# First feed-forward of a four-layer gated block: steps in another order, and w1 applied to inputs split into three bf16 planes

## The chip, the cores and the metric

The kernel runs on one core of one Trainium2 chip. The metric is the device time of one execution of the whole program, in microseconds. The core's engines work from queues of their own and meet at semaphores: TensorE (PE; its weight loads are listed as PEld), VectorE (DVE), ScalarE (ACT), GpSimd (POOL) and SyncE (SP).

## The reference, cut to what matters

The program is four layers, each a cross-attention and a feed-forward, on `x` of 4 x 1024 x 256 in f32. The change lies in the feed-forward of layer 0, which quantises its inputs to 8 bits, its weights to -1, 0 and 1, and has a convolution over three neighbouring positions between its two products:

```python
def act_quant(x):
    scale = 127.0 / jnp.clip(jnp.max(jnp.abs(x), axis=-1, keepdims=True), 1e-05)
    return jnp.clip(jnp.round(x * scale), -128, 127) / scale

def weight_quant(w):
    scale = 1.0 / jnp.clip(jnp.mean(jnp.abs(w)), 1e-05)
    return jnp.clip(jnp.round(w * scale), -1, 1) / scale

def bit_linear(x, w):
    xq = x + jax.lax.stop_gradient(act_quant(x) - x)
    wq = w + jax.lax.stop_gradient(weight_quant(w) - w)
    return jnp.einsum('bsd,hd->bsh', xq, wq)
...
h = bit_linear(x, w1)                                   # 256 -> 1024
h = depthwise_conv1d(h.transpose(0, 2, 1), conv_w, conv_b)   # over positions
...                                                     # silu
return bit_linear(h, w2)                                # 1024 -> 256
...
x = x + jnp.tanh(g_ffn[0]) * _L0_ffn_ref(_layernorm(x, axis=-1), L0_ffn_w1, L0_ffn_conv_w, L0_ffn_conv_b, L0_ffn_w2)
```

## The kernel before, in words

The program runs stage after stage. The one changed is `stage_l0_ffn` (from L213), which runs from about 184 to 453 us. It works through B = 4 batches of 1024 positions (S), each of TB = 8 row tiles of 128 positions, T = 32 tiles in all. The hidden size of 1024 is cut into M = 8 slices of 128. A slot g (0 to 31) is one slice of one batch: b = g // 8, m = g % 8.

What is done to a slot, with hidden channels on the partitions and positions along the row:
- `up(g, half)` (L372, PE): the slice of w1 (128x128, f32, kept as f32 though its values are -1, 0, 1) against the turned inputs `xt` (f32), 512 positions a half, into the PSUM bank `hb[g % 2]`.
- `centre(g)` (L471, ACT): the middle tap of the convolution and its bias, 1024 columns. `conv(g, tap)` (L304 and L306, DVE): the two outer taps, 1023 columns each. `silu(g)` (L477, ACT): into ring buffer `z` of 16 slots.

What is done to a tile t, one tile per step and LAG = 9 steps behind the slots, so that all eight slices of its batch are there:
- `turn_z(t)` (L388, PE): eight 128x128 transposes into PSUM. `largest_hidden(t)` (L311 to L316, DVE): the largest absolute value of each row, and two scales from it. `quantise(t, half)` (L483, ACT): four slices each into `zq`, rounded by adding a large constant.
- `turn_back(t, half)` (L402, PE): four transposes. `copy_q(t, half)` (L490, ACT): to bf16 in `q2`. `down(t)` (L414, PE): eight bf16 matmuls of 256 columns with w2. `update(t)` (L321, DVE): onto the residual. `stats(t)` (L209, DVE): sums for the next layer norm.

What prepares the inputs of the next batch, beside the slots of this one: in slots m < 4 `norm` (L449, ACT) and `largest_input` (L278, DVE), two tiles a step; in slots m >= 4 `quantise_x` (L456, ACT), `dequantise` (L291, DVE), `turn_x` (L362, PE), `copy_x` (L463, ACT), two tiles a step. For batch 0 these run ahead of the first slot, followed on DVE by `norm_range` (L146 to L153), the mean and the reciprocal deviation of the other 24 tiles. `turn_x`, `turn_back` for half 0 and for half 1 share one PSUM bank, `back`.

Each engine runs its list of calls step by step, written out by hand in the loops at the end of its block; an engine never runs anything ahead of its list. In a step of index g the slot g is put through `up`, slot g - 1 through `centre`, `conv` and `silu`; tile t = g - 9 is turned, and tile t - 1 turned back and multiplied by w2. From tile TAIL = 24 on no slots are left (the drained tail, steps 33 to 42); there tiles alternate between two sets of PSUM banks, and PE does `turn_z(t)` ahead of `turn_back(t-1)`:

```python
if 0 <= t - 1 < T:
    copy_q(t - 1, 0)
    copy_q(t - 1, 1)
...
if 0 <= t < T:
    quantise(t, 0)
    quantise(t, 1)
```

This is ScalarE's order around the change. GpSimd has nothing to do in this stage. `round_weights` (L799), in the program's first stage, rounds w1 to -1, 0, 1.

## Time and profile before

| | |
|---|---|
| median of 3 runs | 1910.52 us (1905.21, 1910.52, 1912.49) |
| profiled execution | 1910.83 us, span in the profile 1909.0 us |
| granted TensorE clock, mean | 0.942 |
| busy over the span | PE 1644.5 us (86%), DVE 1159.0 (61%), ACT 882.7 (46%), POOL 321.8 (17%) |
| the changed stage | about 184 to 453 us |

A time is in microseconds from the start of the span. A row of a list names the engine, the line of the code, the operation, the tile written, the tiles read and their shapes; "x8" is eight instructions listed as one. In square brackets stands how long the engine had been idle and what released it. f32 matmuls of 512 columns stand with two records each. The clock that the chip grants TensorE is given as a share of its full 2.4 GHz; 0.50 is the lower level of 1.2 GHz.

### The profile page before, as it was taken

What the parts mean: (1) busy time and instruction counts of PE and PEld (TensorE: products, weight loads), DVE (VectorE), ACT (ScalarE), POOL (GpSimd) and SP (SyncE); (2) the same over time, 40 slices, a digit from 0 to 9 for tenths busy, and PEclk for the clock granted to TensorE, in tenths of its full rate; (3) what the DMA queues carried; (4) which work ended last, traced back from release to release, by engine and by line L of the source; (5) the groups of instructions that cost most, each with busy time, mean ns of one, the idle gap of its engine ahead of it and who ended that gap; (6) DMA issues with size and microseconds to landing.
All of it is one profiled execution on the core that took longest, in us unless ns stands there. A gap on an engine that the chain in (4) does not pass through costs nothing. (4 is left out here: it accounts for less than half of the span.)

```text
span 1909.0 us, 29587 instructions
## 1 busy us (share of the span) xinstructions
PE 1644.5 (86%) x10149; PEld 1246.8 (65%) x10149; DVE 1159.0 (61%) x2579; ACT 882.7 (46%) x1795; POOL 321.8 (17%) x359
## 2 busy tenths in 40 slices
PE   7797788887899898799997399999936999979998
...
GB/s 200 1 1 1 1 1 1 1 1 127 1 1 1 1 1 1 31 1 1 2 1 195 291 65 73 73 70 73 70 196 28 1 2 1 2 47 1 0 1 89
DMA packets 62849, 78.83 MB, mean 41 GB/s; under 512 B 13179, under 2 KB 52655, under 8 KB 62319
## 3 DMA queue, kind: packets, MB, share of 16 engines
...
## 5 line engine op out<-in xcount | busy, mean ns | idle before, releaser
L3002 PEld LDWEIGHTS moe_bank<-moe_xt,moe_w1e 128*128 128x128 f32 x1264 | 155.0, 194 | 5.7 <-DVE moe_xt L2850 1.8
L3002 PE MATMUL moe_bank<-moe_xt,moe_w1e 128*128 128x128 f32 x1264 | 155.8, 277 | 1.1 <-DVE moe_xt L2850 1.1
L3012 PE MATMUL moe_bank<-moe_w,moe_xin 128*128 x632 | 149.3, 379 | 0.0
L3076 ACT ACTIVATE moe_xin<-moe_bank,moe_b 128x128 f32<-128x128 f32 x316 | 90.3, 368 | 124.9 <-PE moe_bank L3002 124.9
L372 PE MATMUL l0f_hb<-l0f_xt,f_w 128*128 128x512 f32 x256 | 125.7, 623 | 5.3 <-DVE l0f_a L306 3.8
L1471 POOL TENSOR_TENSOR all_x<-all_x,l1x_fbias 128x256 f32<-128x256 f32 x32 | 23.3, 732 | 589.9 <-DVE l1x_fxn L204 589.9
L3012 PEld LDWEIGHTS moe_bank<-moe_w,moe_xin 128*128 128x128 f32 x632 | 114.0, 190 | 12.3
L209 DVE BATCH_NORM_STATS2 all_stats<-all_x 128x6 f32<-128x256 f32 x256 | 104.0, 421 | 5.2
L2859 DVE TENSOR_TENSOR moe_y<-moe_bank,moe_b2r 128x256 f32<-128x256 f32 x79 | 33.5, 424 | 118.8 <-PE moe_bank L3012 118.8
L2919 POOL DMA_INDIRECT moe_results<-moe_y,moe_row x79 | 78.0, 988 | 125.1 <-DVE moe_y L2859 121.8
L2850 DVE COPY moe_xt<-moe_bank 128x256 f32<-128x256 f32 x79 | 33.5, 424 | 106.6 <-PE moe_bank L2990 106.6
L2086 PE MATMUL l3f_bank<-l3f_xt,l3f_wx 128*128 128x512 f32 x192 | 87.8, 608 | 0.0
L3067 ACT ACTIVATE moe_w1e<-moe_w 128x1024 f32 x79 | 83.4, 1057 | 3.2 <-issue 2.0
L2914 POOL DMA_INDIRECT moe_xin<-moe_inputs,moe_token x79 | 76.8, 972 | 26.3 <-PE moe_bank L2990 21.6
L2526 PE MATMUL l3x_o_bank<-l3x_vrow,l3x_pt 128*128 128x136 f32 (+1 forms) x640 | 81.2, 282 | 0.0
L2526 PE MATMUL l2x_o_bank<-l2x_vrow,l2x_pt 128*128 128x136 f32 (+1 forms) x640 | 80.6, 281 | 0.0
L372 PEld LDWEIGHTS l0f_hb<-l0f_xt,f_w 128*128 128x128 f32 x256 | 46.9, 200 | 48.4 <-issue 46.3
L2526 PEld LDWEIGHTS l3x_o_bank<-l3x_vrow,l3x_pt 128*128 128x128 f32 (+1 forms) x640 | 77.3, 191 | 0.4
L304 DVE SCALAR_TENSOR_TENSOR l0f_a<-l0f_hb,l0f_cw,l0f_a 128x1023 f32<-128x1023 f32 x32 | 41.0, 1282 | 59.4 <-ACT l0f_a L471 59.4
L2526 PEld LDWEIGHTS l2x_o_bank<-l2x_vrow,l2x_pt 128*128 128x128 f32 (+1 forms) x640 | 76.4, 190 | 0.5
L2164 ACT ACTIVATE l3f_gate<-l3f_bank,l3f_cols 128x512 f32<-128x512 f32 x36 | 24.7, 687 | 105.4 <-PE l3f_bank L2094 105.4
L2008 DVE TENSOR_TENSOR l3f_prod<-l3f_gate,l3f_ct 128x512 f32<-128x512 f32 x12 | 8.3, 692 | 94.4 <-ACT l3f_gate L2164 94.4
...
## 6 DMA issues: line engine op xcount, KB each, us to landing
...
```

The lines of the kernel that those rows point to most:

```text
L209: return nc.vector.bn_stats(sh.stats[:, ds(t * 6, 6)], x_tile(sh, t))
L304: k.link(nc.vector.scalar_tensor_tensor(a[:, u, 1:S], h[:, 0:S - 1], cw[:, m, 0:1], a[:, u, 1:S], ALU.mult, ALU.add))
L372: ins = nc.tensor.matmul(hb[g % 2][:, half * 512:(half + 1) * 512], w1[:, d, m * P:(m + 1) * P], xt[:, b % 2, d, half * 512:(half + 1) * 5 ...
L2086: ins = nc.tensor.matmul(bank[3 * m + k][:, :], wx[:, k, c, m * P:(m + 1) * P], xt[:, c, b * S + j * G:b * S + (j + 1) * G], start=(c == 0 ...
L2526: ins = nc.tensor.matmul(o_bank[:, m * VW:(m + 1) * VW], pt[0:rows(i), u, n, j * P:(j + 1) * P], vrow[0:rows(i), ds((t // TB) * (DC * NV * ...
L2850: nc.vector.tensor_copy(xt[:, u, :], bank[3 * u][:, 0:D]).then_inc(s.et_ready, 1)
L2914: nc.gpsimd.indirect_dma_start(out=gathered(t), out_offset=None, in_=xnd, in_offset=bass.IndirectOffsetOnAxis(ap=token[:, t:t + 1], axis=0 ...
L2919: nc.gpsimd.indirect_dma_start(out=ys, out_offset=bass.IndirectOffsetOnAxis(ap=row[:, t:t + 1], axis=0), in_=y[:, u, :], in_offset=None).t ...
L3002: ins = nc.tensor.matmul(out, w1e[:, at:at + P], xt[:, u, c * P:(c + 1) * P], start=(c == 0), stop=(c == DC - 1))
L3012: ins = nc.tensor.matmul(bank[4 + u][:, 0:D], ht[:, u, c * P:(c + 1) * P], w2[:, ds(e * (HC * D) + c * D, D)], start=(c == 0), stop=(c == ...
L3067: nc.scalar.activation(w1e[:, u * DC * HID:(u + 1) * DC * HID], w1[:, ds(e * (DC * HID), DC * HID)], ACT.Copy).then_inc(s.w1e_ready, 1)
L3076: ins = nc.scalar.activation(ht[:, u, m * P:(m + 1) * P], bank[1 + u][:, m * P:(m + 1) * P], ACT.Gelu, bias=b1[:, ds(e * HC + m, 1)])
```

## The change

- w1 is rounded into a bf16 tile `w1b` (`round_weights`).
- The turned inputs go to `xt` as f32 (now one buffer for one batch) and are split exactly into three bf16 planes `xs`: the rounded value, the rounded rest, the rest of the rest. `up` does six bf16 matmuls a half (two slices of the inputs by three planes), and waits for its own half of the planes.
- Batch 0 is split by ACT (first plane beside the copy, `middle`) and DVE (`rest`, `low`), ahead of `norm_range`; the other twelve pairs of tiles by GpSimd, four operations each, in a chain.
- A step now turns back and multiplies tile t - 2 in place of t - 1 on PE, `turn_z(t)` stands at the end of the step, and there is one step more. `zq` has two buffers. DVE begins a step with `largest_hidden(t-1)`, and `update` and `stats` work on t - 3. ACT has `centre` ahead of `quantise_x`, and `quantise(t-1)` between the two `copy_q(t-2)`.

The diff, cut to its core:

```diff
+        xt = s.sb("xt", [P, DC, S])
+        xs = s.sb("xs", [P, 2, 3, DC, S], BF16)
+        zq = s.sb("zq", [P, 2, 2, HM * P])
...
+                def rest(t):
+                    dve.wait_ge(s.xt_ready, t + 2)
+                    nc.vector.tensor_tensor(rows(t), rows(t), plane(t, 0), ALU.subtract).then_inc(s.rest_ready, 2)
+
+                def low(t):
+                    dve.wait_ge(s.mid_ready, t + 2)
+                    nc.vector.tensor_tensor(plane(t, 2), rows(t), plane(t, 1), ALU.subtract).then_inc(s.xs_ready, 2)
+
                 for t in range(TB):
                     dequantise(t)
+                for t in range(0, TB + 2, 2):
+                    if t < TB:
+                        rest(t)
+                    if t >= 2:
+                        low(t - 2)
                 norm_range(nc, c, sh, TB, T)
...
-                for g in range(END + 3):
+                for g in range(END + 4):
...
-                    if 0 <= t - 2 < T:
-                        update(t - 2)
+                    if 0 <= t - 1 < T:
+                        largest_hidden(t - 1)
+                    if 0 <= t - 3 < T:
+                        update(t - 3)
                     if 1 <= g <= SLOTS:
                         conv(g - 1, 0)
                         conv(g - 1, 1)
...
-                    if 0 <= t < T:
-                        largest_hidden(t)
...
+            @block.gpsimd
+            def _(pool):
+                k = Chain(pool, s.split_step)
+                for t in range(TB, T, 2):
+                    pool.wait_ge(s.xt_ready, t + 2)
+                    if t % TB == 0 and t >= 2 * TB:
+                        pool.wait_ge(s.h_ps, (t // TB - 1) * M)
+                    k.link(nc.gpsimd.tensor_copy(plane(t, 0), rows(t)))
+                    k.link(nc.gpsimd.tensor_tensor(rows(t), rows(t), plane(t, 0), ALU.subtract))
+                    k.link(nc.gpsimd.tensor_copy(plane(t, 1), rows(t)))
+                    nc.gpsimd.tensor_tensor(plane(t, 2), rows(t), plane(t, 1), ALU.subtract).then_inc(s.xs_ready, 2)
...
                 def up(g, half):
                     b, m = g // M, g % M
+                    pe.wait_ge(s.xs_ready, b * TB + (half + 1) * TB // 2)
                     if half == 0:
-                        pe.wait_ge(s.xt_ready, (b + 1) * TB)
                         if g >= 2:
                             pe.wait_ge(s.conv_ready, g - 1)
                     for d in range(DC):
-                        ins = nc.tensor.matmul(hb[g % 2][:, half * 512:(half + 1) * 512], w1[:, d, m * P:(m + 1) * P],
-                                               xt[:, b % 2, d, half * 512:(half + 1) * 512], start=(d == 0), stop=(d == DC - 1))
+                        for k in range(3):
+                            ins = nc.tensor.matmul(hb[g % 2][:, half * 512:(half + 1) * 512], w1[:, d, m * P:(m + 1) * P],
+                                                   xs[:, b % 2, k, d, half * 512:(half + 1) * 512],
+                                                   start=(d == 0 and k == 0), stop=(d == DC - 1 and k == 2))
...
-                    if t > TAIL and t < T:
-                        turn_z(t, 0)
-                        turn_z(t, 1)
-                    if 0 <= t - 1 < T:
-                        turn_back(t - 1, 0, fed)
+                    if 0 <= t - 2 < T:
+                        turn_back(t - 2, 0, fed)
                     if g < SLOTS:
                         up(g, 0)
-                    if 0 <= t - 1 < T:
-                        turn_back(t - 1, 1, fed)
-                    if 0 <= t <= TAIL:
-                        turn_z(t, 0)
-                        turn_z(t, 1)
+                    if 0 <= t - 2 < T:
+                        turn_back(t - 2, 1, fed)
                     if g < SLOTS:
                         up(g, 1)
                     if b < B - 1 and m >= HM:
-                        turn_x(fed, max(0, 2 * t))
+                        turn_x(fed, max(0, 2 * (t - 1)))
                         fed += 2
-                    if 0 <= t - 1 < T:
-                        down(t - 1)
+                    if 0 <= t - 2 < T:
+                        down(t - 2)
+                    if 0 <= t < T:
+                        turn_z(t, 0)
+                        turn_z(t, 1)
...
                 def copy_x(t):
                     act.wait_ge(s.xt_ps, t + 2)
+                    if t < TB:
+                        nc.scalar.activation(pair(plane(t, 0)), turned(t), ACT.Copy)
+                    else:
+                        act.wait_ge(s.xs_ready, t - TB + 2)
+                    nc.scalar.activation(pair(rows(t)), turned(t), ACT.Copy).then_inc(s.xt_ready, 2)
+
+                def middle(t):
+                    act.wait_ge(s.rest_ready, t + 2)
+                    nc.scalar.activation(plane(t, 1), rows(t), ACT.Copy).then_inc(s.mid_ready, 2)
...
+                    if 1 <= g <= SLOTS:
+                        centre(g - 1)
                     if b < B - 1 and m >= HM:
                         quantise_x((b + 1) * TB + 2 * (m - HM))
                         quantise_x((b + 1) * TB + 2 * (m - HM) + 1)
-                    if 1 <= g <= SLOTS:
-                        centre(g - 1)
+                    if 0 <= t - 2 < T:
+                        copy_q(t - 2, 0)
                     if 0 <= t - 1 < T:
-                        copy_q(t - 1, 0)
-                        copy_q(t - 1, 1)
+                        quantise(t - 1, 0)
+                        quantise(t - 1, 1)
+                    if 0 <= t - 2 < T:
+                        copy_q(t - 2, 1)
...
-                    nc.vector.tensor_scalar(f.w1[:, :, :], f.w1[:, :, :], -1.0, None, ALU.max)
+                    nc.vector.tensor_scalar(f.w1b[:, :, :], f.w1[:, :, :], -1.0, None, ALU.max)
```

How this moves instructions, at three places. Names: `l0f_zt` and `l0f_hb0` hold a turned tile, `l0f_back` and `l0f_hb1` the one turned back, `l0f_q2` is what `down` reads.

ScalarE in the drained tail, before: both `copy_q` (L490) of a tile stand ahead of the two `quantise` (L483) of the next.

```order
L490 ACTIVATE l0f_q2<-l0f_back 128x512
L490 ACTIVATE l0f_q2<-l0f_hb1 128x512
L483 ACTIVATE l0f_zq<-l0f_zt,l0f_sc2 128x512 x2
L490 ACTIVATE l0f_q2<-l0f_back 128x512
L490 ACTIVATE l0f_q2<-l0f_hb1 128x512
L483 ACTIVATE l0f_zq<-l0f_hb0,l0f_sc2 128x512 x2
```

After:

```order
L533 ACTIVATE l0f_q2<-l0f_back 128x512
L526 ACTIVATE l0f_zq<-l0f_zt,l0f_sc2 128x512 x2
L533 ACTIVATE l0f_q2<-l0f_hb1 128x512
L533 ACTIVATE l0f_q2<-l0f_back 128x512
L526 ACTIVATE l0f_zq<-l0f_hb0,l0f_sc2 128x512 x2
L533 ACTIVATE l0f_q2<-l0f_hb1 128x512
```

The second `copy_q` of a tile has moved behind the `quantise` of the next tile.

VectorE in a step with inputs (m >= 4), before: the taps (L304, L306), `dequantise` (L291), `largest_hidden` (L311 to L316), `stats` and `update`.

```order
L304 SCALAR_TENSOR_TENSOR l0f_a<-l0f_hb0,l0f_cw,l0f_a 128x1023
L306 SCALAR_TENSOR_TENSOR l0f_a<-l0f_hb0,l0f_cw,l0f_a 128x1023
L291 TENSOR_SCALAR f0_xn<-f0_xn,f0_inv1 128x256 x2
L311 TENSOR_REDUCE l0f_am2<-l0f_zt 128x1
L313 TENSOR_SCALAR l0f_am2<-l0f_am2 128x1
L315 RECIPROCAL l0f_sc2<-l0f_am2 128x1
L316 TENSOR_SCALAR l0f_inv2<-l0f_am2,f0_wmean 128x1
L209 BN_STATS all_stats<-all_x 128x6
L321 SCALAR_TENSOR_TENSOR all_x<-l0f_yb,l0f_inv2,all_x 128x256
```

After:

```order
L333 TENSOR_REDUCE l0f_am2<-l0f_zt 128x1
L335 TENSOR_SCALAR l0f_am2<-l0f_am2 128x1
L337 RECIPROCAL l0f_sc2<-l0f_am2 128x1
L338 TENSOR_SCALAR l0f_inv2<-l0f_am2,f0_wmean 128x1
L343 SCALAR_TENSOR_TENSOR all_x<-l0f_yb,l0f_inv2,all_x 128x256
L326 SCALAR_TENSOR_TENSOR l0f_a<-l0f_hb0,l0f_cw,l0f_a 128x1023
L328 SCALAR_TENSOR_TENSOR l0f_a<-l0f_hb0,l0f_cw,l0f_a 128x1023
L300 TENSOR_SCALAR f0_xn<-f0_xn,f0_inv1 128x256 x2
L209 BN_STATS all_stats<-all_x 128x6
```

`largest_hidden` (L333 to L338) has moved ahead of the taps (L326, L328) and works on the tile turned in the step before.

VectorE at the opening of the stage, before: the eight `dequantise`, then `norm_range`.

```order
L291 TENSOR_SCALAR f0_xn<-f0_xn,f0_inv1 128x256 x8
L146 TENSOR_TENSOR all_var<-all_stats 128x24
```

After:

```order
L300 TENSOR_SCALAR f0_xn<-f0_xn,f0_inv1 128x256 x8
L304 TENSOR_TENSOR l0f_xt<-l0f_xt,l0f_xs 128x2x256 x2
L308 TENSOR_TENSOR l0f_xs<-l0f_xt,l0f_xs 128x2x256
L304 TENSOR_TENSOR l0f_xt<-l0f_xt,l0f_xs 128x2x256
L308 TENSOR_TENSOR l0f_xs<-l0f_xt,l0f_xs 128x2x256
L304 TENSOR_TENSOR l0f_xt<-l0f_xt,l0f_xs 128x2x256
L308 TENSOR_TENSOR l0f_xs<-l0f_xt,l0f_xs 128x2x256 x2
L146 TENSOR_TENSOR all_var<-all_stats 128x24
```

`rest` (L304) and `low` (L308) of four pairs stand between the two.

## Rows read from the trace of the kernel before

**Rows 1.** The costly groups by form, stage alone, 184 to 452.8 us.

```profile
L372 PE MATMUL l0f_hb<-l0f_xt,f_w 128*128 128x512 f32 x256 | 125.7, 623 | 5.3 <-DVE l0f_a L306 3.8 <-ACT l0f_xt L463 1.5
```

**Rows 2.** In order of time (start, duration): `centre` of five slots, last statistics.

```profile
199.00 1.20 ACT L471 ACTIVATE l0f_a<-l0f_hb,l0f_cb,l0f_cw 128x1024 f32<-128x1024 f32 x1 [0.77 <-PE l0f_hb L372]
...
240.98 1.20 ACT L471 ACTIVATE l0f_a<-l0f_hb,l0f_cb,l0f_cw 128x1024 f32<-128x1024 f32 x1
...
300.05 1.22 ACT L471 ACTIVATE l0f_a<-l0f_hb,l0f_cb,l0f_cw 128x1024 f32<-128x1024 f32 x1
...
360.16 1.21 ACT L471 ACTIVATE l0f_a<-l0f_hb,l0f_cb,l0f_cw 128x1024 f32<-128x1024 f32 x1
...
412.74 1.20 ACT L471 ACTIVATE l0f_a<-l0f_hb,l0f_cb,l0f_cw 128x1024 f32<-128x1024 f32 x1
...
452.34 0.43 DVE L209 BATCH_NORM_STATS2 all_stats<-all_x 128x6 f32<-128x256 f32 x1
```

**Rows 3.** The same list, a step without inputs.

```profile
312.20 1.27 ACT L483 ACTIVATE l0f_zq<-l0f_zt,l0f_sc 128x512 f32<-128x512 f32 x2 [0.41 <-DVE l0f_sc L315]
...
312.94 0.65 PE L402 MATMUL l0f_back<-all_ident,l0f_zq 128*128 128x128 f32 x4 [0.25 <-ACT l0f_zq L483]
...
314.59 1.28 DVE L304 SCALAR_TENSOR_TENSOR l0f_a<-l0f_hb,l0f_cw,l0f_a 128x1023 f32<-128x1023 f32 x1 [0.88 <-ACT l0f_a L471]
...
317.11 1.22 DVE L311 TENSOR_REDUCE l0f_am<-l0f_zt 128x1 f32<-128x1024 f32 x1
...
318.74 0.68 DVE L278 TENSOR_REDUCE f_am<-f_xn 128x2 f32<-128x512 f32 x1
318.75 1.26 ACT L483 ACTIVATE l0f_zq<-l0f_zt,l0f_sc 128x512 f32<-128x512 f32 x2 [0.41 <-DVE l0f_sc L315]
```

**Rows 4.** The same list, a step with inputs.

```profile
343.46 0.91 ACT L456 ACTIVATE f_xn<-f_xn,f_sc 128x256 f32<-128x256 f32 x2
...
348.02 0.61 DVE L291 TENSOR_SCALAR f_xn<-f_xn,f_inv 128x256 f32<-128x256 f32 x2
...
350.63 0.48 DVE L321 SCALAR_TENSOR_TENSOR all_x<-l0f_yb,l0f_inv,all_x 128x256 f32<-128x256 f32 x1
```

**Rows 5.** The same list, the drained tail.

```profile
434.44 1.04 PE L388 MATMUL l0f_zt<-all_ident,l0f_z 128*128 128x128 f32 x8
...
436.45 0.59 ACT L490 ACTIVATE l0f_q<-l0f_hb 128x512 bf16<-128x512 f32 x1
...
437.16 1.26 ACT L483 ACTIVATE l0f_zq<-l0f_zt,l0f_sc 128x512 f32<-128x512 f32 x2
437.18 1.03 PE L414 MATMUL l0f_hb<-f_w2q,l0f_q 128*128 128x256 bf16 x8 [0.83 <-ACT l0f_q L490]
...
438.05 1.04 PE L388 MATMUL l0f_hb<-all_ident,l0f_z 128*128 128x128 f32 x8
```

**Rows 6.** The same list, first and last operation of `norm_range` at the opening.

```profile
187.91 0.19 DVE L146 TENSOR_TENSOR all_var<-all_stats 128x24 f32<-128x24 f32 x1
...
191.60 0.18 DVE L153 SCALAR_TENSOR_TENSOR all_shift<-all_mean,all_rstd 128x24 f32<-128x24 f32 x1
```

**Rows 7.** Lines of GpSimd in other stages: duration in ns, min/median/max.

```profile
L886 POOL COPY l0x_rhs<-l0x_crest x4: 607/608/636, 39.6 to 49.4; 128x512 f32<-128x512 f32 x4
...
L2067 POOL TENSOR_TENSOR l3f_prod<-l3f_gate x16: 1263/1768/1772, 1715.9 to 1870.4; 128x512 f32<-128x512 f32 x16
```

**Rows 8.** A pause; two stretches: PE, PEld, DVE, ACT, POOL busy, granted clock.

```profile
226.73 0.63 PE L362 MATMUL l0f_back<-all_ident,f_xn 128*128 128x128 f32 x4 [2.45 <-DVE f_xn L291]
...
226.00:232.00 6.00, 5.27 (x12) 2.42 (x12) 2.58 (x5) 3.54 (x5) 0.00 (x0) 0.72 0.00 0
...
432.00:440.00 8.00, 6.31 (x55) 5.48 (x53) 5.72 (x13) 5.14 (x9) 0.00 (x0) 1.00 0.00 1
```

**Rows 9.** In order of time, GpSimd and VectorE together, in layer 1.

```profile
752.44 0.72 POOL L1471 TENSOR_TENSOR all_x<-all_x,l1x_fbias 128x256 f32<-128x256 f32 x1 [0.44 <-DVE l1x_fxn L204]
...
752.56 0.63 DVE L148 TENSOR_TENSOR all_mean<-all_stats 128x8 f32<-128x8 f32 x1
```

More of the change, by code:

```diff
@@ L228, in stage_l0_ffn @@
         norm_sems(s)
-        w1, w2, w2q, wscale, wmean = f.w1, f.w2, f.w2q, f.wscale, f.wmean
+        w1, w2, w2q, wscale, wmean = f.w1b, f.w2, f.w2q, f.wscale, f.wmean
         xn, am, sc, inv1 = f.xn, f.am, f.sc, f.inv1
@@ L248, in stage_l0_ffn, with rows, plane @@
         tg = sh.gates[:, 4:5]
+        def rows(t):
+            j = t % TB
+            return xt[:, :, j * P:(j + 2) * P]
+        def plane(t, k):
+            b, j = t // TB, t % TB
+            return xs[:, b % 2, k, :, j * P:(j + 2) * P]
         def z_bank(t):
@@ L344, in _ @@
                             input_scales(b + 1)
-                    if 0 <= t - 2 < T:
-                        stats(t - 2)
+                    if 0 <= t - 3 < T:
+                        stats(t - 3)
                     if g == 2:
@@ L401, in turn_back @@
                     for i in range(HM):
-                        ins = nc.tensor.transpose(back_bank(t, half)[:, i * P:(i + 1) * P], zq[:, half, i * P:(i + 1) * P], sh.ident[:, :])
+                        ins = nc.tensor.transpose(back_bank(t, half)[:, i * P:(i + 1) * P], zq[:, t % 2, half, i * P:(i + 1) * P], sh.ident[:, :])
                     ins.then_inc(s.back_ps, 1)
@@ L456, in quantise_x, with turned, pair @@
                     nc.scalar.activation(xn[:, j, :], xn[:, j, :], ACT.Copy, bias=MAGIC, scale=sc[:, j:j + 1]).then_inc(s.q1_ready, 1)
+                def turned(t):
+                    return back[:, :].rearrange("p (t c n) -> p t c n", t=2, n=P)
+                def pair(ap):
+                    return ap.rearrange("p c (t n) -> p t c n", n=P)
                 def copy_x(t):
-                    b, j = t // TB, t % TB
                     act.wait_ge(s.xt_ps, t + 2)
-                    if b >= 2 and j == 0:
-                        act.wait_ge(s.h_ps, (b - 1) * M)
-                    nc.scalar.activation(xt[:, b % 2, :, j * P:(j + 2) * P].rearrange("p c (t n) -> p t c n", n=P),
-                                         back[:, :].rearrange("p (t c n) -> p t c n", t=2, n=P), ACT.Copy).then_inc(s.xt_ready, 2)
+                    if t < TB:
[6 more added lines that the diff above has]
+                    nc.scalar.activation(plane(t, 1), rows(t), ACT.Copy).then_inc(s.mid_ready, 2)
                 def centre(g):
@@ L494, in _ @@
                     quantise_x(t)
-                for t in range(0, TB, 2):
-                    copy_x(t)
+                for t in range(0, TB + 2, 2):
+                    if t < TB:
+                        copy_x(t)
+                    if t >= 2:
+                        middle(t - 2)
                 act.wait_ge(s.small_loaded, 32)
@@ L516, in _ @@
                         silu(g - 1)
-                    if 0 <= t < T:
-                        quantise(t, 0)
-                        quantise(t, 1)
                     if b < B - 1 and m >= HM:
```

15 lines of the change are left out of this document (7 added, 8 removed).

## The prediction

> **What bounds the kernel now.** I first asked the table of costly groups restricted to the stage (184.3 to 452.8 us) what the changed matmuls amount to: 256 f32 records of w1, 125.7 us [rows 1]. The change takes work from these, so the question is whether TensorE sets the time. The list in order of time says it does not. The `centre` starts [rows 2] cut the stage into batches: 199.00 (slot 0), 240.98 (slot 7), 300.05 (slot 15), 360.16 (slot 23), 412.74 (slot 31); the last statistics end at 452.34 + 0.43 = 452.77. Inside a plain step [rows 3] the loop runs through ScalarE and VectorE: `quantise` at 312.20 on ScalarE and `centre` behind it, two `conv` taps on VectorE from 314.59, `largest_hidden` at 317.11, the next `quantise` at 318.75: 6.55 us a step. TensorE waits in it: `turn_back` starts at 312.94 after 0.25 us idle for `zq`. Its own work (two `turn_back` of about 0.45, two halves of `up` of 1.71 = 4 x 0.43, `turn_z` 0.87, `down` 0.87, the last two by the starts in rows 5) is 6.0 of the 6.55. In the drained tail [rows 5] nothing of `up` is left, and a tile takes 438.05 - 434.44 = 3.61 us. I cost the change by the loops it leaves.
>
> **Part 1: bf16 planes in `up`.** Four records of 0.43 us become six bf16 matmuls of 512 columns. `down` does eight of 256 bf16 columns in 0.87 us (437.18 to 438.05), so 0.109 each, 0.216 for 512: 6 x 0.216 = 1.30 in place of 1.71 a half, 27 us less TensorE work over 64 halves. It counts only where TensorE ends the wait, nearly nowhere now (about 0.5 us idle per plain step already). I book it at nothing by itself: the loops of ScalarE and VectorE cover it.
>
> **Part 2: the new order of a step.** Call Z the end of `turn_z`. Now a tile goes: Z, `largest_hidden` and scales 1.64 (317.11 to 318.75), `quantise` x2 1.26, `copy_q` second half 0.59, `down` 0.87 until `turn_z` may start, `turn_z` 1.04: 5.40, with two hops 5.5 us. This is the floor of every step, since PE's queue holds `turn_z(t)` behind `down(t-2)`, which needs `copy_q(t-2,1)`, which stands on ScalarE behind `quantise(t-1)`.
> - Plain steps: VectorE needs 1.64 + `update` 0.48 + `conv` 2.52 (314.59 to 317.11) + `largest_input` 0.68 + `stats` 0.43 (452.34) = 5.8 against 6.55 now [rows 2 to 4]. Without inputs (batch 3) 5.6.
> - Input steps: Z, 1.64, `update` 0.4, `conv` 2.52, `dequantise` 0.61, `turn_x` 0.44 (four transposes where `turn_z` has eight), `down` 0.87, `turn_z` 1.04 and hops: 7.6 us [rows 3, 4, 5]. A batch of before has 59 to 60 us in eight steps [rows 2], with plain steps of 6.55, so about 8.4 for an input step.
> - The first slot of a batch waits for the last pair's split on GpSimd: two casts and two subtractions. The nearest rows are COPY 0.608 and TENSOR_TENSOR 1.263 to 1.772 us, all 128x512 f32 [rows 7]; 2 x 0.61 + 2 x 1.7 + hops = 5 us, from about 0.9 before Z. That makes this step about 7.3 us. Bounds: 3.9 us (two at 1.26) and 6 us (bf16 operands strided), 1 us each way and three times.
>
> **Sum by batches**, at the fast clock, new against the marks of before [rows 2]:
> - Opening: four pairs are copied twice (+0.5 each), `rest`, `middle`, `low` of the last pair (0.7 + 0.6 + 0.7, estimates by the 0.68 of a VectorE pass over 512 columns and the 0.59 of a ScalarE copy of as many [rows 3, 5]), and `norm_range` (187.91 to 191.78, 3.9 us [rows 6]), which now stands behind them on VectorE and no longer beside `turn_x`, partly beside the table load and weight copy: **+4.3**.
> - Slot 0 to 7: four `quantise_x` pairs, 0.91 long [rows 4], leave the path before `centre`, where they cost 0.8 each, and the step into slot 3 gains about 0.4: 41.98 becomes 38.4, **-3.6**.
> - Slot 7 to 15: 59.07 becomes 6.75 (late pair) + 15.3 (to the fourth `turn_z`) + 4 x 7.63 - 1.0 (a `centre` lies 1 us before Z) = 51.6, **-7.4**.
> - Slot 15 to 23: 60.11 becomes 7.3 + 2 x 5.8 + 6.5 (with the input scales) + 4 x 7.63 = 55.9, **-4.2**.
> - Slot 23 to 31: 52.58 becomes 7.3 + 7 x 5.6 + 1.1 = 47.6, **-5.0**.
> - Slot 31 to the end: now 40.03. New: nine steps of 5.5 between tiles 22 and 31, 1.9 before them (`down`, `turn_z`) and 6.4 for the last tile's way out: 57.8, **+17.8**. Here is the price of the reordering. Before, `copy_q` (436.45) stands ahead of `quantise` (437.16) and `down` starts at 437.18 beside it [rows 5]; tiles overlap and 3.61 is enough. Now `copy_q(t-2,1)` waits for `quantise(t-1)`, hence for `largest_hidden(t-1)`, and the tail has no `conv` to fill this with.
> - Together +4.3 - 3.6 - 7.4 - 4.2 - 5.0 + 17.8 = **+1.9 us**.
>
> **Part 3: the clock.** TensorE stood idle for 2.45 us up to 226.73, and the granted clock of 226 to 232 is 0.72, part of the time on 1.2 GHz, part on 2.4 [rows 8]. In the tail of before TensorE is busy 6.31 of 8 us at 1.00 [rows 8]. In the new tail it works 0.9 + 0.87 + 1.04 of 5.5 us and stands idle some 2.7 at a stretch. At 1.2 GHz `down` and `turn_z`, both on the loop, take about twice as long: up to +1.65 a step, 9 steps, 0 to +15; I take +10, since this pause is longer than the one ahead of the slow stretch. The thinner `up` also leaves longer pauses in batch 0 and after the late pairs: 0 to +12, I take +4. So **+14**.
>
> **Part 4: VectorE beside GpSimd.** Twelve splits of 5 us now run beside VectorE. One row speaks for a price: a subtraction-like TENSOR_TENSOR of 8 columns on VectorE took 0.63 us while GpSimd's of 256 columns ran (752.44 to 753.16) [rows 9]; other VectorE operations of 24 columns take 0.18 to 0.19 [rows 6]. Long `conv` taps read PSUM as well, and nothing in the trace shows them beside GpSimd. Bounds: nothing, and a wait of up to a whole GpSimd subtraction (1.7) for one small VectorE operation on the loop in half of the 12 splits, +10. I take nothing for the forecast and let the rival carry it. The Trainium skill (SBUF — State Buffer, "two separate sides") says that GpSimd and a VectorE operation in a two-port mode or with two SBUF inputs exclude each other for a whole instruction. By that rule `dequantise` and the small scale operations would wait; the 0.63 us agrees with it, though a single row can't tell a lock from slower sharing. The skill also gives (GPSIMD Engine Reference, "Elementwise — side-by-side cycle accounting") 4497 ns for a 2048-column f32 `tensor_tensor`; scaled, an estimate of 1.12 us for 512 columns, by which the three late pairs would cost some 1 us less each. The trace has 1.26 to 1.77 for 512 columns [rows 7], and it decides.
>
> **Forecast.** 1910.5 + 1.9 + 14 = **1926.5 us**. The profiled execution took 1910.83 us (span 1909.0), within 0.3 of the median of the runs, 1910.52, so the difference carries over unscaled. About 0.5%, 9.6 us, can be told from no change here.
>
> **Rivals.**
> - *TensorE is the bound after all*. Then its 27 us come off, less part of the opening, and with the tail half as dear: about 1890 us. For it: 6.0 of 6.55 us busy. Against: TensorE's wait in the plain step ends with `quantise` [rows 3], in the tail with `copy_q` [rows 5], and the tail has no `up` to save. It decides if the tail's period stays under 4 us. Chance 0.13 (this holds every way of coming out faster by over 0.5%, a cheaper batch phase included).
> - *The clock stays*: my orders hold, but TensorE keeps 2.4 GHz in the tail. Pauses of 0.83 us within 432 to 440 cost no clock [rows 5, 8]. Then only +1.9: 1912.5 us. Chance 0.27.
> - *The VectorE/GpSimd collision is real*: forecast plus 10: 1936.5 us. For it: the 0.63 us row. Chance 0.2.
> - *Forecast*: 0.40.
>
> **How the numbers follow.** Range: the lower end takes in the clock rival less the uncertainty of the loops and GpSimd's lower bound (1912.5 - 9 = 1903); the upper the collision and the clock's upper end in part (1943). The TensorE rival is left outside, with a little above 1943. Faster 0.13; same 0.27; slower 0.60.
>
> **What would show it.** Right: turns of the tail 5.5 to 7.1 us apart, with TensorE idle until `copy_q` and the granted clock under 0.9 there; first `centre` near 203.3; `largest_hidden` directly after `turn_z`; plain steps near 5.8 and input steps near 7.6; one wait for GpSimd in the first slot of each batch from 1 on. Wrong: a tail of about 3.6 us a tile; input steps that stay at 8.4 or batches that shrink by more than 8 us; `conv` taps or `dequantise` longer than 1.28 and 0.36 us beside the splits; a GpSimd subtraction over 2 us.

## The result, and the profile after

The changed kernel takes 1918.08 us (median of 8 runs, 1914.53 to 1920.43), the kernel before 1911.57 (8 runs, 1905.21 to 1913.49). The ratio is 1.0036, 95% interval 1.0023 to 1.0049: about 6.5 us slower. The direction was forecast, and 1918 lies inside the range, but a loss of 15 to 16 us was forecast and 6.5 came.

Spans of single executions can't be compared to a few us here. Ahead of the stage both kernels run the same code (but for the tile that `round_weights` writes), yet the last statistics before it start at 182.19 us in the profile of before and at 178.42 in that of after; over all the profiles below this start lies between 176.19 and 182.19. So I measure inside the stage, from the start of those statistics to the end of its own last ones. The segments are differences of `centre` starts. First these marks of the changed kernel, in the list in order of time (they answer to [rows 2]):

```profile
198.87 1.19 ACT L514 ACTIVATE l0f_a<-l0f_hb,l0f_cb,l0f_cw 128x1024 f32<-128x1024 f32 x1
...
237.74 1.20 ACT L514 ACTIVATE l0f_a<-l0f_hb,l0f_cb,l0f_cw 128x1024 f32<-128x1024 f32 x1
...
289.91 1.20 ACT L514 ACTIVATE l0f_a<-l0f_hb,l0f_cb,l0f_cw 128x1024 f32<-128x1024 f32 x1
...
344.31 1.20 ACT L514 ACTIVATE l0f_a<-l0f_hb,l0f_cb,l0f_cw 128x1024 f32<-128x1024 f32 x1
...
390.54 1.19 ACT L514 ACTIVATE l0f_a<-l0f_hb,l0f_cb,l0f_cw 128x1024 f32<-128x1024 f32 x1
...
456.14 0.43 DVE L209 BATCH_NORM_STATS2 all_stats<-all_x 128x6 f32<-128x256 f32 x1
```

The segments in us, of all kernels run (those of the experiments are explained below):

| kernel | opening | slots 0-7 | 7-15 | 15-23 | 23-31 | 31 to end | stage |
|---|---|---|---|---|---|---|---|
| before | 16.81 | 41.98 | 59.07 | 60.11 | 52.58 | 40.03 | 270.6 |
| changed | 20.45 | 38.87 | 52.17 | 54.40 | 46.23 | 66.03 | 278.2 |
| forecast for it, clock apart | +4.3 | 38.4 | 51.6 | 55.9 | 47.6 | 57.8 | +1.9 |
| e1_tail_copies | 20.45 | 38.93 | 52.17 | 54.44 | 46.23 | 44.34 | 256.6 |
| e2_all_copies | 20.46 | 38.93 | 53.05 | 55.72 | 46.24 | 42.69 | 257.1 |
| e3_order_only | 17.13 | 38.38 | 50.96 | 55.36 | 49.22 | 70.34 | 281.4 |
| e4_planes_only | 20.46 | 41.91 | 60.17 | 59.92 | 52.38 | 40.18 | 275.0 |
| e5_filled_pause | 20.47 | 38.91 | 52.16 | 54.42 | 46.23 | 59.27 | 271.5 |
| e6_tail_turn_first | 20.45 | 38.65 | 52.16 | 54.41 | 46.22 | 37.82 | 249.7 |
| e7_opening | 20.26 | 38.91 | 52.16 | 54.42 | 46.23 | 42.97 | 255.0 |
| e8_dequantise_first | 20.45 | 42.21 | 49.70 | 51.95 | 46.23 | 42.97 | 253.5 |
| e9_together | 19.40 | 39.00 | 49.11 | 51.94 | 46.22 | 36.34 | 242.0 |
| e10_order_only_tail | 16.91 | 38.37 | 50.97 | 55.35 | 49.23 | 43.48 | 254.3 |
| e11_order_tail_dequantise | 17.27 | 40.88 | 47.43 | 52.06 | 48.68 | 45.06 | 251.4 |

Times of the whole program and of the stage don't agree to the microsecond: e1 has a median 20.2 us under its runs of before and a stage 14.0 us shorter than before's, e4 is 1.5 us over and its stage 4.4 us longer. The profiles are of one execution each, and what differs outside the stage was not looked into. Of the changed kernel the fastest of the eight runs was profiled (1914.53 us).

In the costly groups of the stage after, `up` stands at 99.5 us, 26 less than in [rows 1], so the work did go:

```profile
L407 PE MATMUL l0f_hb<-l0f_xs,f_w1b 128*128 128x512 bf16 x384 | 99.5, 404 | 13.8 <-DVE l0f_a L328 8.3
```

The change gained 22.1 us in the four segments with slots and gave 26.0 back in the tail and 3.6 at the opening. The small result is the difference of two large ones. A tail tile of the changed kernel, in the same list (against [rows 5]):

```profile
436.65 1.87 PE L450 MATMUL l0f_yb<-f_w2q,l0f_q 128*128 128x256 bf16 x8 [2.71 <-ACT l0f_q L533]
438.31 1.71 PE L424 MATMUL l0f_zt<-all_ident,l0f_z 128*128 128x128 f32 x8
...
440.06 1.22 DVE L333 TENSOR_REDUCE l0f_am<-l0f_zt 128x1 f32<-128x1024 f32 x1 [4.37 <-PE l0f_zt L424]
...
441.70 1.26 ACT L526 ACTIVATE l0f_zq<-l0f_zt,l0f_sc 128x512 f32<-128x512 f32 x2 [0.61 <-DVE l0f_sc L337]
...
442.86 0.60 ACT L533 ACTIVATE l0f_q<-l0f_hb 128x512 bf16<-128x512 f32 x1
443.60 1.87 PE L450 MATMUL l0f_hb<-f_w2q,l0f_q 128*128 128x256 bf16 x8 [2.71 <-ACT l0f_q L533]
```

This round is 6.95 us, and it is serial: `down`, `turn_z`, `largest_hidden`, `quantise`, the second `copy_q`, `down`. TensorE stands idle 2.71 us in it, and its `down` and `turn_z` take 1.87 and 1.71 us where they took 1.03 and 1.04. From one `turn_z` to the next the tail's rounds take between 5.48 and 7.06 us. At the full clock, a little earlier, the same round is 5.49 us (404.97 - 399.48):

```profile
399.48 1.03 PE L450 MATMUL l0f_yb<-f_w2q,l0f_q 128*128 128x256 bf16 x8 [1.78 <-ACT l0f_q L533]
...
404.97 1.34 PE L450 MATMUL l0f_yb<-f_w2q,l0f_q 128*128 128x256 bf16 x8 [1.78 <-ACT l0f_q L533]
```

GpSimd's list for the last pair of batch 1, and TensorE's wait for it:

```profile
237.91 0.61 POOL L382 CAST l0f_xs<-l0f_xt 128x512 bf16<-128x512 f32 x1 [1.93 <-ACT l0f_xt L503]
238.60 1.16 POOL L383 TENSOR_TENSOR l0f_xt<-l0f_xt,l0f_xs 128x512 f32<-128x512 f32 x1
...
240.58 1.15 POOL L385 TENSOR_TENSOR l0f_xs<-l0f_xt,l0f_xs 128x512 bf16<-128x512 f32 x1
...
241.79 4.39 PE L407 MATMUL l0f_hb<-l0f_xs,f_w1b 128*128 128x512 bf16 x12 [3.33 <-POOL l0f_xs L385]
```

A split takes 3.8 us, since the subtraction takes 1.16 us and not the 1.26 to 1.77 of [rows 7]. The first four of those sixteen subtractions take 1.26 to 1.32 us. The other twelve take 1.77, and each starts about 0.05 us after a VectorE TENSOR_TENSOR of the same size, as here in the list of before:

```profile
1746.09 0.69 DVE L2008 TENSOR_TENSOR l3f_prod<-l3f_gate,l3f_ct 128x512 f32<-128x512 f32 x1 [7.92 <-ACT l3f_gate L2164]
1746.14 1.77 POOL L2067 TENSOR_TENSOR l3f_prod<-l3f_gate 128x512 f32<-128x512 f32 x1 [9.47 <-ACT l3f_gate L2164]
```

So the 1.77 goes with a VectorE operation that had just begun; no subtraction of a split took over 1.17 here. After its wait of 3.33 us TensorE has a granted clock of 0.50 from 241.79 to 244.40. The opening, in order of time (against [rows 6]): `norm_range` now runs from 193.89 to 197.77, behind the last `low`, and `norm` waits 1.14 us for it ahead of the first `centre`:

```profile
193.89 0.19 DVE L146 TENSOR_TENSOR all_var<-all_stats 128x24 f32<-128x24 f32 x1
...
197.59 0.18 DVE L153 SCALAR_TENSOR_TENSOR all_shift<-all_mean,all_rstd 128x24 f32<-128x24 f32 x1
...
197.87 1.09 ACT L482 ACTIVATE f_xn<-all_x,all_shift,all_rstd 128x256 f32<-128x256 f32 x2 [1.14 <-DVEq L318]
```

And an input step (against [rows 4]): it takes 7.70 us, with TensorE waiting 1.87 us for `dequantise` behind the two taps, then `turn_x`, `down` and `turn_z` in a row:

```profile
272.54 0.61 DVE L300 TENSOR_SCALAR f_xn<-f_xn,f_inv 128x256 f32<-128x256 f32 x2
...
273.30 0.63 PE L396 MATMUL l0f_back<-all_ident,f_xn 128*128 128x128 f32 x4 [1.87 <-DVE f_xn L300]
273.76 1.04 PE L450 MATMUL l0f_yb<-f_w2q,l0f_q 128*128 128x256 bf16 x8
...
274.63 1.04 PE L424 MATMUL l0f_zt<-all_ident,l0f_z 128*128 128x128 f32 x8
```

### The profile page after: what moved, and what is told of

Its sections match the earlier page's. It is cut to its first block and busy times, and to the rows that moved or that the text cites. A ratio compares the mean times of both kernels' runs of the same rounds, so it can differ in the third digit from the quotient of the medians.

```text
span 1912.7 us, 29928 instructions
## 1 busy us (share of the span) xinstructions
PE 1624.4 (85%) x10277; PEld 1247.0 (65%) x10277; DVE 1163.3 (61%) x2587; ACT 884.7 (46%) x1803; POOL 364.2 (19%) x407
## 5 line engine op out<-in xcount | busy, mean ns | idle before, releaser
L407 PE MATMUL l0f_hb<-l0f_xs,f_w1b 128*128 128x512 bf16 x384 | 99.5, 404 | 13.8 <-DVE l0f_a L328 8.3
L407 PEld LDWEIGHTS l0f_hb<-l0f_xs,f_w1b 128*128 128x128 bf16 x384 | 38.7, 103 | 56.5 <-issue 19.4
L2133 PEld LDWEIGHTS l3f_bank<-l3f_xt,l3f_wx 128*128 128x128 f32 x192 | 36.9, 198 | 41.2 <-issue 41.0
```

Of the source, the lines that this page charges most:

```text
L407: ins = nc.tensor.matmul(hb[g % 2][:, half * 512:(half + 1) * 512], w1[:, d, m * P:(m + 1) * P], xs[:, b % 2, k, d, half * 512:(half + 1) ...
L2133: ins = nc.tensor.matmul(bank[3 * m + k][:, :], wx[:, k, c, m * P:(m + 1) * P], xt[:, c, b * S + j * G:b * S + (j + 1) * G], start=(c == 0 ...
```

## The experiments

**1. The tail: ScalarE's order, or TensorE's?** In the drained steps `copy_q(t-2,1)` goes back ahead of `quantise(t-1)`; nothing else is changed.

```diff
                     if 0 <= t - 2 < T:
                         copy_q(t - 2, 0)
+                        if g > SLOTS:
+                            copy_q(t - 2, 1)
                     if 0 <= t - 1 < T:
                         quantise(t - 1, 0)
                         quantise(t - 1, 1)
-                    if 0 <= t - 2 < T:
+                    if 0 <= t - 2 < T and g <= SLOTS:
                         copy_q(t - 2, 1)
```

> The changed kernel, but ScalarE runs both copy_q of tile t-2 ahead of quantise(t-1) in the drained steps (g > 32). Theory A (ScalarE's order makes the tail dear: down(t-2) waits for copy_q(t-2,1), which stands behind quantise(t-1)): a tail tile takes about 3.2 us (a tile's way of 6.3 us shared by two tiles in flight) in place of 5.5 to 6.95, TensorE keeps the full clock, slot 31 to the end falls from 66.0 to about 39 us, and the time from 1918 to about 1891. Theory B (TensorE's own order, turn_z(t) behind down(t-2), with one tile more in flight, sets the tail): the tail keeps 5.5 us or more a tile and the time stays near 1918.

Measured: 1892.12 us, ratio to before 0.9900 (0.9877 to 0.9922). The tail falls by 21.7 us. One order of two ScalarE calls turned a kernel that is 1% faster than before into one that is slower. A tile in its list:

```profile
414.47 1.04 PE L424 MATMUL l0f_zt<-all_ident,l0f_z 128*128 128x128 f32 x8
...
416.48 0.59 ACT L533 ACTIVATE l0f_q<-l0f_hb 128x512 bf16<-128x512 f32 x1
...
417.19 1.27 ACT L526 ACTIVATE l0f_zq<-l0f_zt,l0f_sc 128x512 f32<-128x512 f32 x2
417.21 1.03 PE L450 MATMUL l0f_hb<-f_w2q,l0f_q 128*128 128x256 bf16 x8 [0.83 <-ACT l0f_q L533]
...
418.08 1.04 PE L424 MATMUL l0f_hb<-all_ident,l0f_z 128*128 128x128 f32 x8
```

`down` starts beside `quantise` again, as in [rows 5], and a tile takes 3.61 us, to the hundredth what it took before. My 3.2 us was wrong: I had shared the long way between two tiles, but the short round `turn_z`, `turn_back`, `copy_q`, `down`, in this order on TensorE, is 3.61 by itself. Experiment 5 takes this up.

**2. The same in every step.**

```diff
                     if 0 <= t - 2 < T:
                         copy_q(t - 2, 0)
+                        copy_q(t - 2, 1)
                     if 0 <= t - 1 < T:
                         quantise(t - 1, 0)
                         quantise(t - 1, 1)
-                    if 0 <= t - 2 < T:
-                        copy_q(t - 2, 1)
```

> As e1_tail_copies, but in every step. Theory A: the same gain in the tail; in the steps with slots ScalarE's quantise(t-1) would start up to 0.6 us later, but it is not on the loop of the plain and input steps any more, so batches keep 52 to 54 us and the time is 1888 to 1892. Rival: copy_q(t-2,1) waits for turn_back behind up(g,0) on TensorE and holds quantise(t-1) back, so each of the 24 steps with tiles grows by about 0.5 us and the time is about 1900.

Measured: 1894.39 us, ratio 0.9907 (0.9890 to 0.9924). Slots 7 to 23 take 2.2 us more than in e1, batch 3 the same 46.24, so of the rival's half a microsecond in each of 24 steps only a small part is there. So with `up` between the two `turn_back` the new order costs nothing or helps a little; it is only in the tail that it harms.

**3. Which half of the change shortens the batches?** `e3_order_only` has the changed order with f32 inputs and weights, no split and no GpSimd block; `e4_planes_only` has the order of before with planes and splits. Each is one half of the diff above.

> The changed order of steps with the f32 inputs and f32 w1 of before (no planes, no GpSimd work, no split at the opening). Theory A (the order brings the shorter batches, the planes only let TensorE follow): opening 3.6 us shorter than in the changed kernel, input steps 7.7 as there, first slots about 1 us shorter, steps of batch 3 about 6.1 instead of 5.5 because TensorE has 6.0 us of work in them; tail as dear (66 us); time about 1917. Rival (the planes bring the gain in the batches): slots 7 to 15 to 23 to 31 take 59, 60 and 52.6 us as before, the tail 66, and the time is about 1937.

> The order of steps of before with the bf16 planes, the split at the opening and on GpSimd. Theory A (TensorE is not on the loop of before): batches within 1 us of 59, 60 and 52.6 us plus 1 to 2 us for each first slot that waits for GpSimd, opening +3.6, tail 40: about 1918. Rival (TensorE's 27 us come off): batches shorter by 0.85 us a slot, about 53, 54 and 46, and the time about 1893.

Measured: e3 1918.42 us, ratio 1.0043 (1.0025 to 1.0060); e4 1913.76 us, ratio 1.0012 (1.0001 to 1.0023). By segments, e4 keeps the batches of before to within 1.1 us, though its `up` is as short as in the changed kernel (406 and 404 ns a matmul): some 26 us of TensorE work went and no batch became shorter by more than 0.2 us. In its plain step TensorE just waits longer for `quantise`, 0.67 us at 316.74 in place of the 0.25 of [rows 3]:

```profile
315.99 1.26 ACT L529 ACTIVATE l0f_zq<-l0f_zt,l0f_sc 128x512 f32<-128x512 f32 x2 [0.41 <-DVE l0f_sc L337]
...
316.74 0.66 PE L438 MATMUL l0f_back<-all_ident,l0f_zq 128*128 128x128 f32 x4 [0.67 <-ACT l0f_zq L529]
```

And e3 has nearly all of the gain. The planes show in batch 3: its steps take 6.06 us in e3 and 5.49 to 5.62 in the changed kernel. There the new order has freed the loop of ScalarE and VectorE, and TensorE's 6.0 us are the bound; in the list of e3 it goes from `up` to `down` to `turn_z` to `turn_back` without a pause:

```profile
368.10 1.88 PE L372 MATMUL l0f_hb<-l0f_xt,f_w 128*128 128x512 f32 x4
...
369.82 1.04 PE L414 MATMUL l0f_yb<-f_w2q,l0f_q 128*128 128x256 bf16 x8
...
370.70 1.04 PE L388 MATMUL l0f_zt<-all_ident,l0f_z 128*128 128x128 f32 x8
...
371.57 0.60 PE L402 MATMUL l0f_back<-all_ident,l0f_zq 128*128 128x128 f32 x4
```

The planes save 3.0 us there and 1.0 in slots 15 to 23, and cost 3.3 at the opening, 1.2 in slots 7 to 15 and 0.5 in slots 0 to 7. The tail of e3 was expected at 66 us and took 70.3: the same serial round, at a granted clock of 0.78 over this segment where the changed kernel had 0.82. To see their worth without the dear tail, e3 was run again with the edit of experiment 1:

> e3_order_only (f32 inputs and weights, no planes) with e1's order of ScalarE in the tail. Theory A (the planes as a whole are worth nothing: they cost 3.3 us at the opening and save about 3 us in batch 3): tail 3.61 us a tile, the stage about 255 to 256 us against e1's 256.6, time within 3 us of e1's 1892. Rival (the planes are what makes the kernel fast once the tail is mended): 1900 or more.

Measured: 1892.47 us, ratio 0.9904 (0.9887 to 0.9921), stage 254.3 against 256.6 of e1. The granted clock of the tail differs here too (0.96 in e1, 1.00 in e10; e7 and e8, with the tail code of e1 at 1.00, take 42.97 us for it and not 44.34). The planes as a whole are worth nothing that can be measured.

**4. How much of the tail is the clock?** 20 further matmuls fill TensorE's pause; they write to a bank that `turn_z` overwrites and compute nothing.

```diff
+                    if t >= TAIL:
+                        pe.wait_ge(s.conv_ready, SLOTS)
+                        spare = hb[0] if t <= TAIL + 1 or t % 2 else ztb
+                        for i in range(20):
+                            nc.tensor.matmul(spare[:, 0:D], w1[:, 0, 0:P], w2q[:, i % M, :], start=True, stop=True)
                     if 0 <= t - 2 < T:
                         down(t - 2)
```

> The changed kernel with 20 further bf16 matmuls of 256 columns (about 2.2 us) on TensorE ahead of down(t-2) in each drained step, into a PSUM bank that turn_z overwrites: they fill its pause and compute nothing. Theory A (8 us of the dear tail are the lower clock, the rest is the loop of 5.5 us): the granted clock stays near 1.00, every tail tile takes 5.5 us, slot 31 to the end falls from 66.0 to about 58 us, and the time from 1918 to about 1910. Rival (the clock doesn't matter since TensorE waits anyway): 66 us and 1918, or a few us more because the filler delays down.

Measured: 1910.92 us, ratio 0.9999 (0.9988 to 1.0011). Useless work in the pause made the tail 6.8 us shorter and brought the kernel level with before. Stretches of the tail, first of the changed kernel, then of this one (PE, PEld, DVE, ACT, POOL busy; then the granted clock):

```profile
420.00:430.00 10.00, 5.42 (x38) 4.63 (x37) 4.94 (x12) 4.70 (x8) 0.00 (x0) 0.84 0.01 2
430.00:440.00 10.00, 7.29 (x41) 6.33 (x40) 2.47 (x6) 2.35 (x4) 0.00 (x0) 0.69 0.00 0
```

```profile
420.00:430.00 10.00, 8.96 (x81) 7.86 (x80) 4.86 (x12) 4.70 (x8) 0.00 (x0) 1.00 0.01 2
430.00:440.00 10.00, 8.95 (x81) 7.94 (x80) 4.94 (x12) 4.70 (x8) 0.00 (x0) 1.00 0.01 2
```

So the 26.0 us of the tail are 19.2 for the serial round (59.27 - 40.03) and 6.8 for the clock in these two executions. By the tail of e3 the clock can take more in another execution. Of the 19.2, some 3 us stay when ScalarE's order is put back (42.97 in e7 and e8 against 40.03). The drain has one step more than before; that this is the cause was not tested.

**5. A shorter tail round.** On top of e1, TensorE does `turn_z(t)` ahead of `down(t-2)` for t > TAIL, beside `copy_q`.

```diff
+                    if TAIL < t < T:
+                        turn_z(t, 0)
+                        turn_z(t, 1)
                     if 0 <= t - 2 < T:
                         down(t - 2)
-                    if 0 <= t < T:
+                    if 0 <= t <= TAIL:
                         turn_z(t, 0)
                         turn_z(t, 1)
```

> e1_tail_copies with turn_z(t) ahead of down(t-2) on TensorE in the tail. Theory A (e1's tail tile of 3.61 us is one serial round of turn_z, two turn_back, copy_q, down; with turn_z beside copy_q it is bounded by the work of TensorE, 2.65 us, and ScalarE, 2.5 us): about 2.8 us a tile, slot 31 to the end from 44.3 to about 38 us, time from 1892 to about 1886. Rival (another loop, over largest_hidden and quantise, holds it): 3.6 us a tile as in e1, 1892.

Measured: 1888.43 us, ratio 0.9877 (0.9847 to 0.9906); the tail falls from 44.34 to 37.82. A round is 2.74 us (415.50 - 412.76), and TensorE has no pause left in it:

```profile
412.76 1.03 PE L450 MATMUL l0f_hb<-f_w2q,l0f_q 128*128 128x256 bf16 x8
...
413.63 0.60 PE L438 MATMUL l0f_back<-all_ident,l0f_zq 128*128 128x128 f32 x4
414.07 0.60 PE L438 MATMUL l0f_hb<-all_ident,l0f_zq 128*128 128x128 f32 x4
...
414.50 1.04 PE L424 MATMUL l0f_zt<-all_ident,l0f_z 128*128 128x128 f32 x8
...
415.50 1.03 PE L450 MATMUL l0f_yb<-f_w2q,l0f_q 128*128 128x256 bf16 x8
```

Tiles in flight are worth something only once the short round is broken too.

**6. The opening.** On top of e1, `norm_range` ahead of `rest` and `low`, and the f32 copy of a pair first, its first plane cast from that.

```diff
+                norm_range(nc, c, sh, TB, T)
+                dve.sem_inc(s.rstd_ready, 1)
                 for t in range(0, TB + 2, 2):
...
-                norm_range(nc, c, sh, TB, T)
-                dve.sem_inc(s.rstd_ready, 1)
...
-                    if t < TB:
-                        nc.scalar.activation(pair(plane(t, 0)), turned(t), ACT.Copy)
-                    else:
+                    if t >= TB:
                         act.wait_ge(s.xs_ready, t - TB + 2)
                     nc.scalar.activation(pair(rows(t)), turned(t), ACT.Copy).then_inc(s.xt_ready, 2)
+                    if t < TB:
+                        act.wait_ge(s.xt_ready, t + 2)
+                        nc.scalar.activation(plane(t, 0), rows(t), ACT.Copy).then_inc(s.high_ready, 2)
```

> e1_tail_copies with a cheaper opening: norm_range ahead of rest and low on VectorE, and the f32 copy of a pair first, the first plane then cast from it, so that the shared bank is free sooner. Theory A (the planes' 3.6 us at the opening are norm_range standing behind the split, and four pairs copied twice on the turn_x loop): the opening, last statistics to centre(0), falls from 20.45 to about 18.5 us, the time from 1892 to about 1890. Rival (TensorE at the lower clock ends it): 20 us or more, 1892.

Measured: 1891.61 us, ratio 0.9904 (0.9882 to 0.9925), opening 20.26. A miss: the rival's figure came (20 us or more), but its cause, TensorE's lower clock, was not tested, and the list shows another. With `norm_range` first, the first `rest` starts only at 186.01, `middle` stands ahead of the next `copy_x` on ScalarE and waits for it, and `turn_x` waits for the bank:

```profile
186.79 0.63 ACT L508 ACTIVATE l0f_xs<-l0f_xt 128x512 bf16<-128x512 f32 x1 [2.12 <-DVE l0f_xt L304]
187.33 0.58 ACT L501 ACTIVATE l0f_xt<-l0f_back 128x512 f32<-128x512 f32 x1
...
187.96 1.11 PE L396 MATMUL l0f_back<-all_ident,f_xn 128*128 128x128 f32 x4 [2.85 <-ACT l0f_xt L501]
```

The copy order alone, within experiment 8, brings 1.05 us.

**7. The input step, and GpSimd beside VectorE.** On top of e1, the two `dequantise` ahead of the two `conv` on VectorE; and the same on top of e10, where GpSimd has no work.

```diff
+                    if b < B - 1 and m >= HM:
+                        dequantise((b + 1) * TB + 2 * (m - HM))
+                        dequantise((b + 1) * TB + 2 * (m - HM) + 1)
                     if 1 <= g <= SLOTS:
                         conv(g - 1, 0)
                         conv(g - 1, 1)
-                    if b < B - 1 and m >= HM:
-                        dequantise((b + 1) * TB + 2 * (m - HM))
-                        dequantise((b + 1) * TB + 2 * (m - HM) + 1)
```

> e1_tail_copies with dequantise ahead of conv on VectorE. Theory A (the input step of 7.7 us is the serial round turn_z, largest_hidden, update, conv, dequantise, turn_x, down; conv's 2.5 us leave it): input steps of 6.2 to 6.4 us, bounded by ScalarE's work (centre, quantise_x, copy_q, quantise, silu, copy_x), with tiles, and 4.9 in batch 0: slots 7 to 15 and 15 to 23 shorter by 5 us each, 0 to 7 by 2 to 3 us, time from 1892 to about 1880. Rival (the planes on GpSimd or ScalarE's queue hold the step): 7.5 us or more, 1890.

> e10_order_only_tail with dequantise ahead of conv in all steps, the counterpart of e8 without work on GpSimd. In e8 the two dequantise of a step took 0.96 to 1.21 us while GpSimd's TENSOR_TENSOR ran, 0.61 elsewhere. Theory A (VectorE waits for a port or lock that GpSimd's instruction holds): all 24 in pairs of 0.61 us here. Rival (they are longer for another reason, for instance ScalarE reading beside them): 0.9 us or more here too.

Measured: e8 1888.83 us, ratio 0.9895 (0.9869 to 0.9922). Input steps with tiles fall from 7.70 to between 6.82 and 6.88 us, not to the 6.2 to 6.4 expected (what holds them was not settled), but batch 0, which has no tiles, loses 3.3 us. `conv` there stands behind `dequantise`, which waits for `quantise_x`, and behind GpSimd, as shown below. e11 (one run, 1888.03 us) was for the durations. In the list of e8, GpSimd's subtraction and cast and the two `dequantise` beside them:

```profile
269.90 1.16 POOL L383 TENSOR_TENSOR l0f_xt<-l0f_xt,l0f_xs 128x512 f32<-128x512 f32 x1
...
270.67 1.21 DVE L300 TENSOR_SCALAR f_xn<-f_xn,f_inv 128x256 f32<-128x256 f32 x2 [0.22 <-ACT f_xn L489]
...
271.13 0.61 POOL L384 CAST l0f_xs<-l0f_xt 128x512 bf16<-128x512 f32 x1
```

The 16 `dequantise` between 255 and 345 us by their line (ns min/median/max), first in e8, then in e11:

```profile
L300 DVE TENSOR_SCALAR f_xn<-f_xn,f_inv x16: 343/442/752, 264.5 to 336.8; 128x256 f32<-128x256 f32 x16
```

```profile
L291 DVE TENSOR_SCALAR f_xn<-f_xn,f_inv x16: 343/346/351, 259.7 to 332.3; 128x256 f32<-128x256 f32 x16
```

With GpSimd at work beside it a `dequantise` takes up to 0.752 us, without it never over 0.351 (0.356 in the whole stage of e11), and GpSimd's subtraction stays at 1.16. Taken one by one, the first of the pair takes 0.54 us and ends at 271.21, the second takes 0.75, from 271.13 to 271.88. GpSimd's subtraction ends at 271.06 (269.90 + 1.16) and its cast at 271.74, so each `dequantise` ends 0.14 or 0.15 us after the GpSimd operation beside it. Where a `dequantise` starts first, the cast is the one that gets longer: 0.66 us in place of 0.61, twice. The Trainium skill (SBUF — State Buffer, the section on SBUF's two separate sides) says that GpSimd and a VectorE operation in a two-port mode or with two SBUF inputs exclude each other for a whole instruction. These ends agree with it if `dequantise` runs in such a mode, which no view shows. The three small scale operations behind `largest_hidden` take 0.15 to 0.20 us beside a split as elsewhere: my prediction had expected them to wait too.

In steps with tiles this costs little: the four input steps from slot 19 on take 27.9 us in e8 and 27.6 in e11. In batch 0 it lies on the loop. Its pair of `dequantise`, first in e8, then in e11:

```profile
227.87 1.21 DVE L300 TENSOR_SCALAR f_xn<-f_xn,f_inv 128x256 f32<-128x256 f32 x2 [3.10 <-ACT f_xn L489]
```

```profile
226.04 0.75 DVE L291 TENSOR_SCALAR f_xn<-f_xn,f_inv 128x256 f32<-128x256 f32 x2 [3.10 <-ACT f_xn L453]
```

The pair is 0.46 us longer in e8, and so is the step: 6.82 us from one `centre` to the next, 6.36 in e11. Three such steps make 1.4 of the 3.3 us that e8 loses in batch 0. In the changed kernel no `dequantise` of the later batches lies beside a split: its 16 in the same stretch take 344 to 349 ns. Three in batch 0 meet the end of one and take 0.39 to 0.40 us.

**8. What beats both.** e6, with `dequantise` ahead of `conv` only where a tile is in the step too (t >= 1), and the copy order of e7 with `norm_range` left where the change has it.

> e6_tail_turn_first with dequantise ahead of conv only in steps that also have a tile (not in batch 0, where e8 lost 3.3 us), and at the opening the f32 copy of a pair ahead of its first plane, norm_range where the changed kernel has it. By the segments of e1, e6, e8: opening about 19.2 (norm_range ends it, 1.3 us sooner than 20.45), slots 0 to 7 38.9, 7 to 15 49.7, 15 to 23 51.9, 23 to 31 46.2, tail 38: 244 us for the stage against 278.2 in the changed kernel and 270.6 before, time about 1882 to 1885. Rival (the gains share one loop and don't add): no better than e6, 1888.

Measured: 1880.21 us, ratio 0.9828 (0.9814 to 0.9841), 31.9 us under its runs of before, the stage 242.0 us against 244 expected. The gains add up.

## Why the prediction was wrong in size

- **TensorE is not the bound, planes booked at nothing**: right, shown by e4 (1.0012) and e10. The rival that its 27 us come off is out. I hadn't said that after the reordering TensorE would be the bound of batch 3; there the planes did earn 3.0 us.
- **The serial round of 5.5 us in the tail**: right, 5.49 measured, and the order of ScalarE is its cause (e1). +19.2 us against +17.8. Turns 5.5 to 7.1 us apart were named as its sign, 5.48 to 7.06 came.
- **The clock in the tail, +10**: right in kind, 6.8 measured (e5), so mis-sized by 3.2. e5 is also the rival "the clock stays" made real: forecast 1912.5, measured 1910.9.
- **The clock elsewhere, +4** ("the thinner `up` also leaves longer pauses in batch 0 and after the late pairs"): this term failed in size. The clock did fall in batch 0: from slot 0 to 7 it is 0.82 in the changed kernel, 0.92 in the one before and 0.96 in e3. But that stretch came out only 0.5 us above the full-clock sum and 0.5 above e3; TensorE is busy for 24.5 of its 38.9 us, so it had time for slower matmuls. After the first late pair the clock was 0.50 and six matmuls of `up` took about 2.6 us in place of 1.3. At the other two late pairs TensorE waited 0.71 us and kept 1.00. Together some 1.8 us, not 4.
- **The split of 5.0 us on GpSimd**: this term failed too, 3.8 measured. I took 1.7 us for a subtraction from rows of GpSimd beside VectorE, and 6 us as the bound for strided bf16 operands. It took 1.16, with bf16 output 1.15 to 1.16. From one `turn_z` to the next the late step takes 6.09 and 6.10 us in batches 2 and 3 where I had 7.3, which is just the 1.2 that the split is shorter. Against e3, which has no split, it costs nothing there (6.06): TensorE does wait 0.71 us, but its two halves of `up` are 0.4 shorter each. At the first batch boundary the step from `centre` to `centre` takes 6.83 us, 5.59 in e3. The forecast of 6.75 was met by luck: the split was 1.2 shorter and the low clock behind it, which I had booked elsewhere, cost about 1.3. For the subtraction I had the Trainium skill's figure (GPSIMD Engine Reference, "Elementwise — side-by-side cycle accounting", an estimate of 1.12 us) and set a row of another stage against it; for this operation the run agrees with the page.
- **Plain steps**: from the third step of a batch on they take 5.48 to 5.62 us where I had 5.8, 5.6 and 6.5 for the one with the input scales. Starts on VectorE lie up to 0.1 us closer than durations say, and I added durations; that this is all of it was not tested. Slots 15 to 31 came out 2.9 us below the forecast, 2.4 of them by the two splits. Input steps took 7.70 us, not 7.63.
- **Opening +4.3**: 3.6 measured, 0.3 of which e3 has too. The parts that I named add up to 7.9 us, and I hadn't said how much of them the other work hides.
- **Collision with VectorE**: nothing, as taken, but only because three `dequantise` met no more than the end of a split and the others none. Where e8 moved them beside it, the collision was real.

The forecast sum was +15.9 us, the stage moved by +7.6 and the medians by 6.5. The misses are about -1.8 in the tail (+1.4 for the round, -3.2 for its clock), -2.2 for the clock elsewhere, -3.6 for three splits, -0.5 for the plain steps, -0.7 at the opening and +0.6 for the input steps. No term was off by more than 4 us; the gains were forecast at 20 and came to 22, the losses at 36 and came to 30. But the net is their difference, and the errors, nearly all of one sign, doubled it.
